# One period's order on four engines: convolution, B, outer products, third gather, memory and GpSimd's last two states

## What is computed

```python
# layer 0: retention and a four-stage feed-forward net, both on xn = layernorm(x)
q, k, v = xn @ Wq, xn @ Wk, xn @ Wv
s = ((q @ k.T) * gamma ** (i - j), lower triangle) @ v
h = silu(xn @ w1 * s1) * (xn @ w2 * s2)        # z, 512 wide
h = gelu(h @ h1 * h1_s);  h = gelu(h @ h2 * h2_s);  g = h @ w3 * w3_s
# layer 1: selective state space and mixture of depths, both on yn = layernorm(x)
xc = silu(conv4(yn @ W_in[:, :128]));  gate = yn @ W_in[:, 128:]
B, C = split(xc @ W_x)                          # 16 states each
h_t = A * h_(t-1) + xc_t * B_t;   y_t = C_t . h_t + D * xc_t
s = (y * silu(gate)) @ W_out
g = yn + sigmoid(score) * ffn(yn) for the 512 tokens with the highest score
```

## Time and profile before

| | us |
|---|---|
| median of 3 runs | 537.83 (537.45 to 539.37) |
| profiled execution | 537.29 |
| its span, first to last instruction | 535.5 |
| TensorE, matmuls busy | 441.1 (82%) |
| VectorE busy | 394.2 (74%) |
| GpSimd busy | 387.8 (72%) |
| ScalarE busy | 291.4 (54%) |
| mean granted TensorE clock | 0.949 |

### The profile page before, as it was taken

How to read it: one execution, slowest core, us unless ns; L and a number is a source line. 1 busy time by engine, 2 the same in 40 slices (tenths; PEclk the granted TensorE clock), 3 DMA queues, 4 the chain that set the end, 5 groups by cost and what they waited for, 6 DMA issues and landing times.

```text
span 535.5 us, 6095 instructions
## 1 busy us (share of the span) xinstructions
PE 441.1 (82%) x1796; PEld 261.6 (49%) x1807; DVE 394.2 (74%) x683; ACT 291.4 (54%) x475; POOL 387.8 (72%) x317
## 2 busy tenths in 40 slices
PE   0794968898989898998889897989799889875843
PEld 0573645654555555654565455545555457321221
DVE  2282042959779895879688986798698949978985
ACT  3763654685467646763667556764676466333300
POOL 1672561788499859987699859984998679863682
PEclk9996979899999999999999999999999999898865
DMA  8300004421342215320633144312523053306330
GB/s 319 140 21 4 1 1 125 112 78 40 88 110 79 80 35 161 99 80 20 194 84 78 40 138 127 76 54 62 144 73 96 20 159 79 98 23 174 86 91 20
DMA packets 25379, 46.97 MB, mean 88 GB/s; under 512 B 3072, under 2 KB 4096, under 8 KB 25088
## 3 DMA queue, kind: packets, MB, share of 16 engines
q1 hardware_dynamic: 24336, 45.13, 29.9%
q10 hardware_dynamic: 1008, 1.41, 0.8%
HBM read 42.33 MB, written 4.19 MB: 87 GB/s over the span
## 4 chain that ended last, share of the span: by engine, by line
PE 34%; DVE 22%; issue 17%; POOL 16%; ACT 8%; DMA 2%; SPq 0%; DVEq 0%; POOLq 0%; ACTq 0%
PE bank0a L940 18%; DVE hs L1371 9%; DVE xbank L1348 6%; POOL hs L556 6%; PE bank0a L1059 5%; POOL hidAl L518 2%; ACT xn L692 2%; POOL hidBl L518 2%; PE ybank L1085 2%; PE bank1a L1020 2%; POOL g L530 2%; POOL xr L538 1%; POOL q L507 1%; DMA Bt<-w_in 1%; DVE st L1276 1%
## 5 line engine op out<-in xcount | busy, mean ns | idle before, releaser
L556 POOL TENSOR_TENSOR hs<-hs,Ct 128x512 f32<-128x512 f32 x127 | 170.9, 1350 | 34.5 <-DVE hs L1371 22.3
L518 POOL TENSOR_TENSOR hidAl<-plain,hidAh 128x512 fp32r<-128x512 f32 x48 | 63.7, 1327 | 39.3 <-ACT hidAh L651 33.2
L1371 DVE TENSOR_TENSOR_SCAN hs<-decay,carry,xbank 128x512 f32<-128x512 f32 x63 | 80.5, 1278 | 8.0 <-DVE xbank L1348 0.5
L518 POOL TENSOR_TENSOR hidBl<-plain,hidBh 128x512 fp32r<-128x512 f32 x48 | 67.0, 1396 | 26.4 <-ACT hidBh L651 18.5
L1371 DVE TENSOR_TENSOR_SCAN hs<-decay,xbank 128x512 f32<-128x512 f32 x64 | 78.0, 1219 | 5.6 <-DVE xbank L1348 0.5
L1348 DVE TENSOR_TENSOR xbank<-xs,bbank 128x512 f32<-128x512 f32 x104 | 71.5, 687 | 1.3
L650 ACT ACTIVATE plain<-bank0a,col 128x512 f32<-128x512 f32 x64 | 44.1, 689 | 44.7 <-PE bank0a L940 43.5
L940 PE MATMUL bank0a<-hidBh,hTh 128*128 128x512 f32 x128 | 57.8, 452 | 1.7 <-ACT q L683 1.7
L940 PE MATMUL bank0a<-hidAh,hTh 128*128 128x512 f32 x128 | 56.4, 441 | 1.7 <-ACT q L683 1.7
L940 PE MATMUL bank0a<-hidAl,hTh 128*128 128x512 f32 x128 | 51.7, 404 | 0.0
L940 PE MATMUL bank0a<-hidBl,hTh 128*128 128x512 f32 x128 | 50.7, 396 | 0.0
(11 more groups left out here) (190 smaller groups left out, 938.8 us busy)
## 6 DMA issues: line engine op xcount, KB each, us to landing
xs<-x_rows SPq DMA_DIRECT2D x128, 256.0 KB, 3.5
xt<-x_tok SPq DMA_DIRECT2D x8, 256.0 KB, 4.8
xr<-x_feat SPq DMA_DIRECT2D x8, 256.0 KB, 7.6
x_rows<-xc SPq DMA_DIRECT2D x8, 256.0 KB, 2.3
out<-xr SPq DMA_DIRECT2D x7, 256.0 KB, 2.3
fh<-h_w SPq DMA_DIRECT2D x1, 1024.0 KB, 9.6
hs<-h_w SPq DMA_DIRECT2D x1, 1024.0 KB, 11.4
lw<-l_w ACTq DMA_DIRECT2D x1, 640.0 KB, 5.3
```

The source lines that it names most:

```text
L518: pool.tensor_tensor(low[:, m, :], plain[:, k % NPLAIN, :], high[:, m, :].bitcast(F32), ALU.subtract).then_inc(hidden_low, 1)
L556: pool.tensor_tensor(h, h, Ct[:, hs_(u)], ALU.mult).then_inc(p_ready, 1)
L1371: dve.tensor_tensor_scan(hs[:, i % NSTATES, :], decay[:, gr:gr + 1].broadcast_to([P, HALF]), xbank[:], 0.0 if u % 2 == 0 else carry[:, k:k ...
```

## The change

The order of `slot` changes on four engines; no instruction is added or taken away. TensorE: the convolution comes directly behind the transposes, in slot 4; B moves from slot 6 to slot 5, ahead of gate; outer and the gather of quad 2 move from slot 4 to slot 5, between B and gate. ScalarE takes B before gate, and L1_ACT says so. VectorE: memory moves from slot 4 to slot 6, behind the output product, and gate_y of all halves but the last from slot 9 to slot 11. GpSimd, slots 6 to 10: k = 14, add_output; k = 15, rstd_l0, h1 low 0; h1 low 1, k = 0; h1 low 2, k = 1, h1 low 3; k = 2, weigh_update. Before the loop it does two low parts of h1, not three.

```diff
--- before.py
+++ after.py
@@ -150,7 +150,7 @@
         L0_DVE += [("z2", _v, 1), ("scores", _v), ("z2", _v, 3), ("outer", _v)]
     if _n is not None:
         L0_ACT.append(("tok", _n))
-        L1_ACT += [(_k, _n) for _k in ("xnT", "conv", "gate", "B", "C", "score", "score_col")]
+        L1_ACT += [(_k, _n) for _k in ("xnT", "conv", "B", "gate", "C", "score", "score_col")]
     if _v is not None:
         L0_ACT += [("z1", _v, 2), ("z1", _v, 3)] + [("h1", _v, _m) for _m in range(KT)] + [("u", _v)]
     if _w is not None:
@@ -563,23 +563,25 @@
                 if v is not None:
                     if 1 <= s < 1 + KT:
                         low_hidden("z", v, s - 1)
-                    elif 6 <= s < 6 + KT:
-                        low_hidden("h1", v, s - 6)
+                    elif s in (8, 9):
+                        low_hidden("h1", v, s - 7)
                 if w is not None and s == 11:
                     low_xn(w)
                 if v is not None and 11 <= s < 11 + KT:
                     low_hidden("h2", v, s - 11)
                 if n is not None and s == 2:
                     rstd_l1(n)
-                if w is not None and s == 8:
-                    rstd_l0(w)
                 if u is not None:
                     weigh_states(u, k)
+                if w is not None and s == 7:
+                    rstd_l0(w)
+                if v is not None and s in (7, 9):
+                    low_hidden("h1", v, 0 if s == 7 else 3)
                 if v is not None and s == 5:
                     scale_q(v)
                 if s == 6 and e is not None and e != UNITS - 2:
                     add_output(e)
-                if t is not None and s == (1 if t == UNITS - 1 else 6):
+                if t is not None and s == (1 if t == UNITS - 1 else 10):
                     weigh_update(t)
                 if t is not None and s == update_slot(t):
                     add_tokens(t)
@@ -602,7 +604,7 @@
             pool.tensor_scalar(earlier[:, HALF - P:HALF], tri, TINY, None, ALU.mult).then_inc(earlier_ready, 1)
             pool.tensor_tensor(w_conv[:], lw[:, 0:P].rearrange("p (o d) -> p o d", o=1).broadcast_to([P, TAPS, P]),
                                raw_conv, ALU.mult).then_inc(w_conv_ready, 1)
-            for m in range(KT - 1):
+            for m in range(KT - 2):
                 low_hidden("h1", 0, m)
             rstd_l0(1)
             for p in PERIODS:
@@ -794,13 +796,12 @@
                 if n is not None:
                     if s == 5:
                         convolved(n)
+                        take_B(n)
                         take_gate(n)
                 if v is not None and s == 5:
                     hidden("h1", v, 0)
                 if n is not None:
-                    if s == 6:
-                        take_B(n)
-                    elif s == 7:
+                    if s == 7:
                         take_C(n)
                 if v is not None and 6 <= s < 5 + KT:
                     hidden("h1", v, s - 5)
@@ -1124,25 +1125,24 @@
                             retention_q(v)
                         elif s == 2:
                             scores(v)
-                        elif s == 4:
-                            outer(v)
                     if t is not None:
                         for kt in range(KT):
                             if down_slots(t)[kt] == s:
                                 mod_down(t, kt)
                     if n is not None and s == 3:
                         norm_to_features(n)
-                    if s in (1, 4) and t is not None:
-                        gather_y(t, 1 if s == 1 else 2)
+                    if n is not None and s == 4:
+                        convolve(n, (3, 2, 1, 0))
                     if s == 5 and e is not None and e != UNITS - 2:
                         project_out(e)
-                    if n is not None:
-                        if s == 4:
-                            convolve(n, (3, 2, 1, 0))
-                        elif s == 5:
-                            project("gate", n, W_IN[:, P:2 * P])
-                        elif s == 6:
-                            project_x("B", n, W_B)
+                    if n is not None and s == 5:
+                        project_x("B", n, W_B)
+                    if v is not None and s == 5:
+                        outer(v)
+                    if s in (1, 5) and t is not None:
+                        gather_y(t, 1 if s == 1 else 2)
+                    if n is not None and s == 5:
+                        project("gate", n, W_IN[:, P:2 * P])
                     if v is not None and 5 <= s < 5 + KT:
                         hidden("h1", v, s - 5)
                     if n is not None:
@@ -1422,7 +1422,7 @@
                 if v is not None:
                     if s == 2:
                         mask_scores(v)
-                    elif s == 4:
+                    elif s == 6:
                         memory(v)
                 if t is not None:
                     if t % 2 == 0 and compare_slots(t)[CPH] == s:
@@ -1431,7 +1431,7 @@
                         token_weights(t)
                     if t == UNITS - 1 and s == 8:
                         finish_last()
-                    elif t < UNITS - 1 and s == 9:
+                    elif t < UNITS - 1 and s == 11:
                         gate_y(t)
                     if t == UNITS - 1 and s == 0:
                         output(e)
```

## The result

The changed kernel takes **521.62 us** (median of 4 executions, 521.11 to 522.07) where the kernel before, in runs beside it, takes 537.85: a ratio of 0.9693, 95% interval 0.9671 to 0.9715. The profiled execution ran 522.04 us with a span of 520.2, against 537.29 and 535.5. Forecast were 517.6 and a range of 514 to 526.

A forecast was written before the change was run, and what follows sets the result against it. The bound was taken to be h2's late start behind GpSimd's queue order. Gains of 1.0, 2.2, 13.4, 2.2 and 1.4 us, together 20.2, took 537.29 to 517.1; 0.54 for the median made 517.6 us, range 514 to 526.

The forecast's parts named there:

- The four full periods: Periods 2 to 5: h2 starts sooner in each, 4 x 3.35 = 13.4 us gained.
- period 5's gain: h2 of period 5 starts at 385.2 instead of 388.56, 3.35 us sooner.
- the case of ScalarE: Rival: ScalarE's first h1 tile frees its bank 0.7 us late in seven periods, 4.9 us lost, 522.6; chance 0.12.
- Start-up: ... Nothing: Before the loop: h1's low 2 changes places with GpSimd's reciprocal roots, at no gain or loss.
- The cover named there: TensorE stands 4.9 us before its loop, hiding low 2 and 3 (2.5 us); without it 1.3 us.
- Period 0: B out of the row and no C wait, with TensorE at half clock: 1.0 us gained (0.3 to 1.6).
- Period 7: Last convolution starts sooner, at 471.5 instead of 472.88, and VectorE hands the gain on: 1.4 us.
- VectorE's wait in front of the residual: VectorE, idling 2.51 us before the next residual product, arrives over 4 us sooner and waits longer there.
- GpSimd stayed ahead of h2: Rival: slowed GpSimd delivers h1's low 3 0.3 or 1.2 us too late for h2, 519.7 or 523.6; chance 0.10.
- The stop only moves: Rival: memory's wait for outer products delays GpSimd's low parts; at 7 us no gain is left, 537; chance 0.04.
- The clock rival: Rival: TensorE at half clock at convolution and h2 in each of seven periods, 43 us more, 560; chance 0.04.
- The port rule: VectorE two-input and GpSimd operations exclude each other; priced at three 1.30 us products, low 3 0.3 us late, 519.7.

The follow-up runs named there:

- three edits on one row of dependences: Changed kernel plus, cumulatively, VectorE's scan before the slot 0 residual product, masking before the slot 2 scan, GpSimd's roots before z's low part: 518.3, 514.82, 512.09 us.
- roots ahead: Changed kernel with VectorE's scan and score masking moved earlier, and GpSimd's layer-1 reciprocal roots before the z low part: 512.09 us, ratio 0.9497.
- scan and mask: Changed kernel with VectorE's slot 0 scan before the residual product and score masking directly behind the slot 2 statistics: 514.82 us, ratio 0.955.

## Why the prediction was right, and where it wasn't

**The mechanism, right.** Nearly every step in period 5 came out by its own measure: 23.67 us from convolution to h2 (23.6 forecast), 18.75 from convolution to the score transposes (18.7), 0.26 from there to ScalarE's last tile, 4.66 on to h2 (4.67), memory waiting 0.37 us (0.4), 30.95 us from h2 to the end of the unchanged slots as before. Low part 3 starts 21.2 us behind the convolution (21.4 forecast) and is wanted at about 25. The four full periods give 12.84 us where 13.4 were forecast, 0.07 to 0.21 less each: the prediction took period 5's gain for all four, and the even ones give 3.14. One gain in the sum was too large: C to score was to shrink from 3.26 us to 3.0 and shrinks to 3.15 (365.33 to 368.48). And B's new place costs something: from the output projection to the product behind it there are 1.09 us (356.63 to 357.72) where the outer products, in the run with B back in slot 6, come after 0.85. So undoing B's move loses 0.50 us, and not 0.55 to 0.86. Two small slips of the working change nothing: 1.74 less 1.27 is 0.47 and not 0.48, and the case of ScalarE adds up to 522.5.

**The start-up, wrong.** The step that failed is "Start-up: ... Nothing". The cover named there held, but the profiled execution lost 2.75 us before the loop, most or all of it with TensorE's clock, and unchanged code varies by 1.4 us (61.57 and 62.93). The sum was made against one execution, the one with the earliest cut of all fourteen; it should have carried a term for the start of 1 to 2 us on the slower side. Without it the profiled execution would have run 519.3.

**Period 0, mis-sized.** The term was 1.0 us (0.3 to 1.6) and measured 0.28. TensorE is at half clock (1.2 of 2.4 GHz) twice there. Changed kernel, columns as above:

```profile
77.20:84.60 7.40, 6.16 (x12) 3.25 (x13) 0.75 (x1) 2.68 (x5) 3.76 (x3) 0.54 0.00 0
105.50:108.70 3.20, 3.20 (x9) 2.49 (x8) 3.13 (x5) 1.26 (x2) 1.14 (x2) 0.53 0.24 82
```

The slow stretch of the earlier trace rows ended inside the convolution; now it covers nearly all of it (79.45 to 85.9, for 4.19 us at the full clock), and B waits 0.95 us behind it for xc. The row named the stretch, but the forecast kept the convolution's start and not the clock that it would run at.

**Period 7, mis-sized.** From the w3 product to the last convolution the gain is 1.31 us (15.03 to 13.72; forecast 1.4), and 0.42 is handed back between that convolution and the end (62.62 to 63.04). Where in the tail wasn't traced.

**VectorE's wait in front of the residual**, forecast to grow, did so where it had been short, from 0.99, 1.22 and 1.24 us in periods 2, 4 and 6 to 2.23, 2.49 and 2.52, and hardly in period 5 (2.51 to 2.62). That VectorE arrives there as much sooner as TensorE and no more may stem from its new waits for ScalarE's copy of B, 5.3 us in four places; that wasn't tested. Without effect on the sum.

**The rivals.** ScalarE's bank never made TensorE wait; GpSimd stayed ahead of h2. "The stop only moves" did not occur, but two runs show that it was one edit away: memory in slot 4 gives 535.66, and the old order of GpSimd under the new order of the rest 546.75, which is slower than before. The clock rival did not occur in periods 1 to 6 of the changed kernel in its first two profiled executions (granted 1.00 in each of them); in the third (527.2 us) the clock was at half for some 6 us around the convolution of period 5, which came out 2.9 us longer, and again at the convolution of period 7, with 2.5 us more from there to the end. With the old order of GpSimd it occurred where TensorE waited 2.95 us for a gather. It is a loss in single places and executions, not one in each period as the rival had it.

**The port rule.** The pair of low parts at 366.53 takes 2.97 us (2.5 alone), and beside it stands VectorE's product at 366.95 with 1.42 instead of 0.69. Read as the Trainium skill puts it (SBUF — State Buffer, section "SBUF: two separate sides": of two such operations, whichever starts first holds the port pair that VectorE and GpSimd share for its whole instruction), that fits to 0.25 us: VectorE's product waits for the first low part to end near 367.8, runs 0.69 to 368.5, and the second low part ends 1.25 behind it, at 369.7 (measured 369.50). The prediction priced this rule wrongly, at three whole products of 1.30: of such a product only the 0.7 us that it would take alone is taken from GpSimd, the rest is its own waiting.

## What to carry to other kernels

When an in-order queue stands still in front of an operation, ask which work behind it is already ready, and move that ahead; but price the whole set of moves together, since here one half alone loses 1.65% and one edit of another engine (memory's slot) decides over 2.3%. Cut two traces at a mark that the change doesn't touch and compare period by period before comparing totals: start-up and clock here moved totals by up to 2.75 us, hid a loss of 0.5 us in every or every second period in two runs and lent others a gain that their edits hadn't made. And a wait and a total that both come out as expected don't show the way between them: with memory in slot 4 both did, and most of the loss went another way. A gain in one stage goes up to the next wait and no further: three edits on one row of dependences paid 40, 70 and 30% of what their own waits promised.

## What the runs showed of the hardware that was not expected

The granted clock of TensorE in period 0 has a second slow stretch, some 3.2 us inside h2, that is there or not by kernel: present in both executions of the kernel before, in all three of the changed kernel and in five of the other nine runs (h2 to w3 takes 15.8 us), absent with GpSimd's order alone, memory in slot 4, B in slot 6 and roots ahead (14.3 us in each of the four). It is worth 1.5 us, and no reading of the instructions around it told why. The h2 stage of period 0 with it (scan and mask) and without it (roots ahead):

```profile
101.40:117.30 15.90, 15.87 (x53) 9.40 (x53) 13.05 (x19) 10.28 (x16) 12.69 (x11) 0.89 0.32 86
```

```profile
103.30:117.70 14.40, 14.31 (x53) 8.26 (x53) 13.43 (x19) 10.34 (x17) 12.12 (x10) 1.00 0.32 84
```

A VectorE operation on four elements per lane took 0.57 us where a GpSimd operation ran and 0.17 where none did. In the run with scan and mask it took 0.57 to 1.06 in seven of its eight places, with the roots ahead 0.17 in all eight. So when such an operation stands in a chain, what GpSimd has queued beside it counts.
